# Query product from the transposed raw input, scaled after the product; GpSimd's turn and the setup in another order

## The reference

```
x = x + xattn(layernorm(x), ctx, ctx, mask, Wq, Wk, Wv, bq, bk, bv)   # all ReLU, no softmax
        # qp = relu(q@Wq + bq); s = relu(qp@kp.T)/sqrt(dk) + mask; out = relu(s@vp)
x = x + (quantised(layernorm(x)) @ quantised(W).T + b)                # FP6 grid, scale per 32 elements
x = x + (layernorm(x)@W1.T + mean(ctx)@W2.T + b)
x = x + expert_ffn(layernorm(x))   # each of E experts takes its 128 best tokens, three products
```

## Time and profile before

| | before |
|---|---|
| median of three runs | 744.15 us (743.94 to 744.85) |
| span of the profiled execution | 743.2 us |
| PE busy | 716.2 us (96%) |
| DVE busy | 521.6 us (70%) |
| ACT busy | 401.9 us (54%) |
| POOL busy | 420.4 us (57%) |
| turns 8 to 11 (143.42 to 188.72 us) | 45.30 us |

### The profile page before, as it was taken

One profiled execution on the slowest core, in us unless ns is written; L12 is line 12 of the kernel. 1 busy time (PEld: TensorE's weight loads), 2 busy tenths in 40 slices (PEclk: granted clock), 3 DMA queues, 4 the chain that ended last, 5 costly groups with the idle time before them and its releaser, 6 DMA issues.

```text
span 743.2 us, 12766 instructions
## 1 busy us (share of the span) xinstructions
PE 716.2 (96%) x4513; PEld 624.9 (84%) x4513; DVE 521.6 (70%) x978; ACT 401.9 (54%) x680; POOL 420.4 (57%) x621
## 2 busy tenths in 40 slices
PE   6999999999999999999999799999999999999994
PEld 5765888888888888888888778798999899899894
DVE  5786789889888888876896697464663565463561
ACT  5755444444544545868668334364664656464641
POOL 2825788888888887786788622503521443340132
PEclk9999999999999999999999899999999999999998
DMA  9610121221222213111117898696796698895534
GB/s 317 256 30 15 43 86 62 88 86 58 88 79 82 71 58 108 52 60 44 49 45 264 322 396 279 149 391 186 222 370 185 185 330 293 289 266 167 142 86 58
DMA packets 61671, 118.04 MB, mean 159 GB/s; under 512 B 6056, under 2 KB 7464, under 8 KB 61608
## 3 DMA queue, kind: packets, MB, share of 16 engines
q1 hardware_dynamic: 54312, 100.44, 38.7%
q0 software_dynamic: 7296, 16.78, 10.3%
HBM read 91.76 MB, written 25.21 MB: 157 GB/s over the span
## 4 chain that ended last, share of the span: by engine, by line
PE 84%; issue 6%; DMA 4%; DVE 3%; ACT 2%; POOL 1%; POOLq 0%; SPq 0%; DVEq 0%; ACTq 0%
PE bank L354 39%; PE banks L354 9%; PE bank L361 6%; PE bank L994 6%; PE banks L861 4%; PE banks L867 4%; DMA out<-y,ids 3%; PE banks L871 2%; PE banks L994 2%; PE banks L872 2%; PE banks L1423 1%; PE banks L1028 1%; PE bank L1318 1%; PE bank L1041 1%; DMA out<-x 1%
## 5 line engine op out<-in xcount | busy, mean ns | idle before, releaser
L2844 POOL DMA_INDIRECT out<-y,ids x24 | 46.1, 1922 | 157.4 <-DVE y L2555 155.5
L1973 DVE TENSOR_TENSOR w_l<-w_raw,w_h 128x2048 fp32r<-128x2048 f32 x35 | 80.1, 2291 | 63.2 <-ACT w_h L1496 49.4
L1961 DVE BATCH_NORM_STATS2 bn<-x 128x6 f32<-128x512 f32 x113 | 77.7, 688 | 8.2 <-DMA x<-x 5.4
L1496 ACT ACTIVATE w_h<-w_raw 128x2048 fp32r<-128x2048 f32 x36 | 68.5, 1918 | 7.2 <-DMA w_raw<-w 7.2
L1892 ACT ACTIVATE h<-bank,b 128x512 f32<-128x512 f32 x48 | 33.0, 688 | 62.5 <-PE bank L354 57.8
L1973 DVE TENSOR_TENSOR hT_l<-h,hT_h 128x512 fp32r<-128x512 f32 x48 | 33.0, 689 | 39.8 <-ACT hT_h L1898 37.7
L354 PE MATMUL bank<-tokT_h,w_h 128*128 128x256 f32 x188 | 55.1, 293 | 0.0
L2607 POOL TENSOR_SCALAR rstd<-mean_var 128x1 f32<-128x1 f32 x108 | 25.7, 238 | 50.9 <-DVE mean_var L1966 42.6
L354 PE MATMUL bank<-tokT_h,w_l 128*128 128x256 f32 x188 | 53.2, 283 | 0.0
L354 PE MATMUL bank<-tokT_l,w_h 128*128 128x256 f32 x188 | 53.2, 283 | 0.0
L354 PE MATMUL bank<-wf_h,xdT_h 128*128 128x512 f32 x128 | 52.6, 411 | 0.0
(11 more groups left out here) (419 smaller groups left out, 2380.1 us busy)
## 6 DMA issues: line engine op xcount, KB each, us to landing
w_raw<-w SPq DMA_DIRECT2D x36, 1024.0 KB
early_w<-w SPq DMA_DIRECT2D x24, 1024.0 KB, 10.0
x<-x SPq DMA_DIRECT2D x32, 256.0 KB, 2.7
out<-x SPq DMA_DIRECT2D x32, 256.0 KB, 2.0
xn<-xn SPq DMA_DIRECT2D x32, 256.0 KB
mask<-mask_t SPq DMA_DIRECT2D x8, 256.0 KB, 3.4
slot_all<-slots SPq DMA_DIRECT2D x4, 512.0 KB, 7.8
stage<-wk SPq DMA_DIRECT2D x1, 1024.0 KB, 7.7
```

The costliest lines, as they stand in the source:

```text
L1496: act.activation(dst, src, ACT.Copy).then_inc(sem, 1)
L1961: dve.bn_stats(bn6[which][:, j % 2, :], src[:, :]).then_inc(sem_bn[which], 1)
L1973: dve.tensor_tensor(dst, src, hi_part, ALU.subtract).then_inc(sem, 1)
L2844: pool.indirect_dma_start(out=out_rows, out_offset=bass.IndirectOffsetOnAxis(ap=ids[:, r:r + 1], axis=0), in_=y[e % 2][b][:, :], in_offset ...
```

## The change

The query product no longer starts from the normalised tile. A new input `x_t`, the transposed x, is loaded by SP, 1 MB for a group, and is split on three engines: the high part on ACT (`xt_hi`, two instructions of 128x1024 for a group, in turns k%4 of 0 and 1), the low part half on POOL (two instructions of 128x512, in turns k%4 of 0 and 2) and half on DVE (`xt_lo`, one of 128x1024, in turn k%4 == 2). The mean of each column is taken out of Wq once, in the setup (four matmuls with a matrix of 1/512 on PE, two subtractions on DVE). The product is multiplied by 1/sqrt(var + eps) of its tokens afterwards, by DVE (`scaled`, 128x512 from PSUM, once in a turn), before `q_relu`, which now reads SBUF. The factors come from `rstd1`, now on POOL for four tiles at once, and go by way of DRAM: `store_r1` writes 512 values, `load_rb` reads them back to all partitions. Removed are t1 on PE, norm1 and hi1 on ACT, lo1 on DVE, rstd1 of each tile on POOL, and six small matmuls (`warm_up`) at the start.

In the order of the code: on ACT hi2 now stands ahead of q_relu and norm4(k-3) behind it; on POOL q_lo of a chunk moves from the end of a turn to the next turn, behind rstd_of(1), and rstd_of(3) moves behind x1b; in the setup the transfers of Wq and of the first group of x_t come first and the tiles of x behind those of the context and Wk.

```
         def t1(j):                                # PE, removed
-            pe.wait_ge(sm.a_xn1, j + 1)
...
-            four_transposes(pe, bank1(j), xn1).then_inc(sm.p_t1, 1)
...
+        def xt_lo(g):                             # DVE
+            dve.wait_ge(sm.a_xth, 2 * g + 2)
+            part = slice(0, C) if g < 2 else slice(2, C)
+            lo(sm.d_xtl, xT1[g % 2][1][:, part, :], xt_raw[g % 2][:, part, :], xT1[g % 2][0][:, part, :])
+        def scaled(g, c, n):
+            dve.wait_ge(sm.p_q, n + 1)
...
+                dve.wait_ge(sm.rb_in, 16 * g)
...
+            dve.tensor_tensor(q32[n % 2][:, :], ps_q[n % 2][:, :], rb[:, :], ALU.mult).then_inc(sm.d_z, 1)
...
             j = k + 10                            # DVE, in turn k
             if valid(j) and k >= 2:
                 stats1(j)
+            if q_units(k):
+                scaled(*q_units(k)[0])
+            if k % GRP == 2 and 2 <= (k + 6) // GRP < G:
+                xt_lo((k + 6) // GRP)
             if parts_of(k) is not None:
                 logit_parts(parts_of(k))
...
             if valid(k) and k <= N - 7:           # POOL, in turn k
                 rstd_of(1, k, sm.d_st2, sm.g_r2)
+            if k >= 4 and not drain(k - 1):
+                for unit in q_units(k - 1):
+                    q_lo(*unit)
             if valid(k - 2) and k != 2 and not drain(k):
                 mix_bias(k - 2)
-            if valid(k - 3) and not drain(k):
-                rstd_of(3, k - 3, sm.d_st4, sm.g_r4)
...
             pool.tensor_tensor(x1_of(k)[:, :], x1_of(k)[:, :], fbias[:, :], ALU.add).then_inc(sm.g_x1b, 1)
+            if valid(k - 3) and not drain(k):
+                rstd_of(3, k - 3, sm.d_st4, sm.g_r4)
...
-            if not drain(k):
+            if k < 3:
                 for unit in q_units(k):
                     q_lo(*unit)
+            if valid(k + 10) and (k + 11) % GRP == 0:
+                rstd1((k + 10) // GRP)
+            if pool_piece(k) is not None:
+                xt_lo(*pool_piece(k))
...
+        def load_rb(g):                           # SP
+            sp.wait_ge(sm.r1_out, 16 * g)
+            sp.wait_ge(sm.d_z, GRP * g)
+            sp.dma_start(rb[:, :], rows_on_all(io.r1[g * GT:(g + 1) * GT], GT)).then_inc(sm.rb_in, 16)
```

More of the change, by code:

```diff
@@ L137, in build @@
     bn6 = [place(f"bn{i}", [P, 2, 6]) for i in range(4)]
-    rstd = [place(f"rstd{i}", [P, slots[i], 3]) for i in range(4)]
+    rstd = [None] + [place(f"rstd{i}", [P, slots[i], 3]) for i in range(1, 4)]
+    r1 = place("rstd1_cols", [P, 3, GRP])
     amax = place("amax", [P, NB])
@@ L169, in build @@
     xT1 = [[place(f"xT1_{i}{n}", [P, C, GT], F32R) for n in "hl"] for i in range(2)]
+    xt_raw = [place(f"xT1_{i}raw", [P, C, GT], at=at_xt1 + (2 * i + 1) * 8 * 1024) for i in range(2)]
     at_qt = top[0]
@@ L1031, in early_outputs, with query_weight_means, first_rows @@
                 last.then_inc(sm.p_ev, 1)
+        def query_weight_means():
+            for d in range(C):
+                if d % 2 == 0:
+                    pe.wait_ge(sm.c_wq0 if d == 0 else sm.c_wq1, 16)
+                if d == 0:
+                    pe.wait_ge(sm.g_set, GS["mean"])
+                last = pe.matmul(ps_tb[:, :], mean_w[:, :], stage[0][:, d, :], start=(d == 0), stop=(d == C - 1))
+            last.then_inc(sm.p_set, 1)
+        def first_rows():
+            pe.wait_ge(sm.c_ident, 16)
+            pe.wait_ge(sm.g_r1, 1)
+            for t in range(GRP):
+                last = pe.transpose(ps_ta[:, t * P:(t + 1) * P], r1[:, 0, t:t + 1].to_broadcast([P, P]), ident[:, :])
+            last.then_inc(sm.p_set, 1)
         def keys():
@@ L1758, in _ @@
                 setup("crow")
[L1759 to L1763 removed]
+            if halves_of_group(k) is not None:
+                xt_hi(*halves_of_group(k))
             g = scores_of(k)
@@ L2004, in setup @@
                     .then_inc(sm.d_set, 1)
+            if what in ("wqc0", "wqc1"):
+                half = slice(0, 2) if what == "wqc0" else slice(2, 4)
+                dve.wait_ge(sm.p_set, T["wqm"])
+                lo(sm.d_set, stage[0][:, half, :], stage[0][:, half, :],
+                   ps_tb[:, :].unsqueeze(1).to_broadcast([P, 2, D]))
             if what in ("wq0", "wq1"):
@@ L2306, in _ @@
                 setup("va1")
+                scaled(*q_of(4))
             if valid(k - 2) and k - 2 != N - 1:
                 third_low(k - 2)
-            j = k + 9
-            if valid(j) and k >= 3:
-                lo1(j)
             if k == 1:
```

261 lines of the change are left out of this document (120 added, 141 removed).

## The result

The changed kernel takes 780.72 us (median of four runs, 777.45 to 783.12) against 744.35 us for the kernel before in the same comparison: 1.0482 times as long, 95% interval 1.0455 to 1.0509. The direction was forecast, the size was not: 752.5 us was forecast with a range of 737 to 757. The profiled execution has a span of 781.3 us, 38.1 more than before. It is the slowest of the four (783.12); by the medians the change costs 36.4 us.

The account below looks back on a forecast made before the run. PE's own work was taken to bound the loop. Setup +1.2, turns 4 to 21 (-0.9, +2.6, +5.1, -0.9) and turns 22 and 23 +1.3 gave +8.4 on a 743.2 us span, so 752.5 us; range 737 to 757.

Parts of the forecast that it names:

- The way through DRAM is no term: Loop: load_rb follows a group's last scaled at about +7.5 us, the next needs it over 10 us later; no cost.
- Setup, +1.2 (bounds -3 and +4): Start of turn 4: 1.2 us later through added scaled and xt_lo on DVE, if ACT's casts are in time.
- Turns 4 to 21, +5.9: Loop: -0.9 for turns 4 and 5, +2.6 for 6 and 7, 5.1 for three groups, -0.9 for 20 and 21.
- The mechanism of the score turn: Turns k%4 of 2 and 3: late d_st2 delays ffn 0.3, scores 1.2, attend 1.9 us; the pair costs 2.6 more.
- the 0.35 us of q8: DVE, turn k%4 == 2: q8 waits for POOL's mix_bias, between 0 and 0.75 us; 0.35 taken.
- The rule that the prediction drew from its rows: DVE and POOL: DVE instructions with two operands from SBUF and POOL's wait for each other.
- Xt_lo, which the prediction set at 0 beside POOL: DVE, turn k%4 == 2: xt_lo takes 1.22 us; meeting POOL's short instructions adds 0 to 0.53, taken as 0.
- xd is in time in turns k%4 of 0 and 1: Ordinary turns: POOL's xd ends at 5.4 us, PE reaches t2 at 5.95; narrowly in time, so each turn saves 0.44.
- Every wait at its own length, and PE at full clock throughout: Whole sum: PE's waits added at their lengths, PE read at full granted clock in turns 8 to 11; no clock term.
- Drain and experts untouched: From 326.03 us to the end: the change adds nothing.
- A: Rival, loop: stalls don't come and t1's share remains; 737.0 us, 733 to 741 with the setup's bounds; chance 0.24.
- B: Rival, score turn: DVE isn't late, d_st2 stays at +10.77, only moved rstd_of(3) delays s_lo; 745 to 746 us; chance 0.18.
- C: Rival: POOL and DVE exclude each other at each meeting, 4.6 us more, or setup 4 us late; 757 us; chance 0.10.

Follow-up runs that it names:

- experiment 2: Changed kernel without the stores of the factors of groups 2 to 7, a constant row being read instead; 780.83 us.
- experiment 7: Changed kernel with the factors spread by four PE transposes and an ACT copy per group instead of through DRAM; 770.36 us.
- 1: Changed kernel with SP's setup load of x_t for group 2 issued ahead of the store and read-back of group 1's factors; 781.36 us.
- experiment 12: Experiment 7's kernel with POOL's q_lo(6) moved behind rstd_of(1) and rstd_of(2) in turn 2; 769.44 us.
- experiment 11: Experiment 7's kernel with xt_lo, scaled, rstd_of(3), q_lo and search steps rearranged in the loop, and setup's xt_lo(1), scaled and two statistics behind the values; 766.93 us.
- Experiment 6: Changed kernel with ACT's search steps (settle, probe) behind hi2 and ahead of q_relu and norm4; 779.98 us.

## Why the prediction was wrong

**The way through DRAM is no term.** This is the step that failed most. It was argued from when the next `scaled` needs the row, more than 10 us later. For the loop that was true of the read-back and beside the point: the row was in time, and with the store the tile x issued ahead of it came late. For the setup it was false: there load_rb(1) waits for the store and stands ahead of load_xt(2). Experiments 2 and 7 show the one, 1 and 7 the other, 13.0 us of span together, the clock's part included.

**Setup, +1.2 (bounds -3 and +4).** Measured +12.25, of which 6.8 is the round trip, and +5.45 remains in experiment 7. Of that, 1.3 go by the comparison of 12 with 7 to the clock at 0.50 near 14 us, where before has 1.00 from 9.9 us on. The sum had xt_lo for group 1 at 2.44 us less 1.47 us of idle time, on the condition that ACT's casts are in time. They were not: they stand on ACT behind q_relu, which waits for `scaled`, and DVE waits 1.69 us for them (37.78). Xt_lo takes 2.58 and two more statistics stand ahead of the values, which are at 41.89 instead of 36.51. Where the rest of it lies is only partly tested: experiment 11 moved these instructions and gained 1.7 us at turn 2 and 0.3 at turn 4 over experiment 7.

**Turns 4 to 21, +5.9.** Measured +16.4. Two score turns with a late x are 2.7 and 3.7 of it; t1's 0.44 came as forecast. The mechanism of the score turn was right in each of its three waits, with sizes of 0.66, 1.21 and 2.11 against 0.3, 1.2 and 1.9. The pair costs 3.54 instead of 2.6. The term that was too small is the 0.35 us of q8: it came 1.10 later, since the sum left out rstd1 ahead of the deviation and looked for the meeting with mix_bias at q8, while xrq ahead of it was held. The rule that the prediction drew from its rows names instructions with two operands from SBUF; xrq has one small tensor and one value per partition. Its sentence from the Trainium skill ("SBUF — State Buffer", Who interferes with whom) that a single SBUF input is free leaves out that section's exception, the 2-port modes; whether xrq runs in one no run shows. Xt_lo, which the prediction set at 0 beside POOL, took its 1.22 us; the POOL instruction beside it (the third of rstd_of(3) in turn 14) took 1.45 us, against 0.27 in turn 15. That xd is in time in turns k%4 of 0 and 1 held; in k%4 == 2, which the sum didn't look at, t2 is 0.38 late.

**Every wait at its own length, and PE at full clock throughout.** The sum had no term for the clock. In after it fell to 0.50 in five stretches ahead of the experts, four of them during or soon after a wait of PE, and the longer matmuls are some 7.7 us of the 38.1: 1.3 near 14 us, 1.8 in ffn(0) (4.68 us against 2.87 in experiment 7), 1.5 in turn 11, 1.6 in turn 19 (15.28 us of PE time against 13.71 in turn 15) and 1.5 in turn 25 (12.09 against 10.59 in experiment 2). These are estimates from pairs of stretches at the two clocks.

**Drain and experts untouched.** True from turn 27 on (+0.5). But the search begins in turn 22, inside the loop; 326.03 us is the start of turn 24 in the trace of before, not the end of the loop. Its steps on ACT stand behind q_relu, which the change gives a new wait, and behind norm4, which it moved: +3.34 and +5.67 in turns 22 to 26 against +1.3 and 0. The order of ACT's queue showed it; the term was left out. Experiment 6 gets 3.9 us of it back, the clock included; what keeps the rest is open.

**The rivals.** A fell: PE waits in each score turn. B fell: d_st2 comes at +13.00. C named a late setup and gave it 4 us; most of the cause was another one. Its 0.4 more for q8 came true and was too small. The range ended at 757 because no case had a transfer, the search steps or the clock in it.

The sum by cause, of the 38.1 us of the traced execution, with the clock by itself: the round trip 8.4 (5.0 in the setup, 3.4 in turns 11 and 19); what remains of the setup 4.1; the score turns with t1, by the forecast mechanism, 9.9 (forecast 5.9); turns 22 to 26 7.5; from turn 27 on 0.5; the clock 7.7. Of the clock, 1.8, 1.5 and 1.6 came in the setup and in turns 11 and 19, by the waits of the round trip; with them it is 13. Shown by an edit are the round trip and 2.4 us of turns 22 to 26; the score turns' waits are measured and their edits only moved them.

## What to carry to other kernels

When a change moves work between engines, cost each new transfer by what stands behind it in its queue and by the transfers issued next to it, not only by when its own reader needs it. When a producer gains a wait (here q_relu), list all that its engine does behind it, in every stage of the program, the late ones too. And when engines are nearly full in a turn (PE 10.28, DVE 10.10 and POOL 9.25 of 10.51 us in turn 14), moving one instruction moves the wait: take the edits out together, or count the whole chain.

## What the runs showed of the hardware

**A store of 2 KB in 4-byte pieces takes 8.0 to 10.6 us to land in after** (8.0 in the setup, 8.9 to 10.6 in the loop; the window around turn 10 has 576 packets under 512 B), and a 256 KB tile issued just ahead of it landed after 9.2, 7.6, 2.8 or 2.9 us; without the store (experiment 2) after 2.9 to 3.3. The Trainium skill ("DMA: Bandwidth & Descriptors", Specifications) says that transfers below 512 B make the DMA engines read, modify and write and miss the line rate; the trace agrees in direction. By the same page's fit for one DMA (Anatomy of one DMA, 2.0 us and the bytes at 436 GB/s, for those that GpSimd starts) 2 KB would be an estimate of 2.0 us; the trace, where SP starts the store, has four to five times that.

**A wait on PE can cost more than its length.** In after the granted clock falls to 0.50, the 1.2 GHz level, in four stretches between 30 and 410 us; the rows of them stand among the windows above (0.57 and 0.66 are means over the stretch shown). Before, it is 1.00 from 9.9 to 416 us throughout. In turn 11 PE is idle for 3.11 us to 193.74, the clock is at 0.50 from about 195.3 to 198.7, and PE is busy for 15.18 us instead of 13.71 in turn 15, 1.47 more. Turn 15 of experiment 6, with the same three waits as in after:

```profile
238.33:257.05 18.72, 15.25 (x74) 12.71 (x73) 14.23 (x27) 5.95 (x11) 13.81 (x21) 0.91 0.52 149
```

It takes 18.72 us at a mean clock of 0.91, against 17.18 at 1.00. So the same waits can cost 1.5 us more, and the turns of the versions with waits show this step several times (turn 7 takes 18.72 us in experiment 7 and 17.20 in experiment 12; turn 25, with the same wait of 2.62 us, 14.71 in after and 13.21 in experiment 2). It lies in different turns from trace to trace, so it can be part of why the runs of these kernels differ. What decides whether a wait lowers the clock was not tested.
